# Row maxima of an attention unit moved once for all heads, by SyncE, with the transposed scores half a unit later

## The chip, the cores and the metric

One core of one Trainium2 chip runs the whole program as a single launch. The metric is device time in microseconds (us) from one run to the next of the same program: the median of the runs shown, lower is better. The profile below comes from one more execution, taken by the hardware profiler.

## The reference, cut to what matters

The input is 16 sequences of 256 tokens with 256 features and a context of the same shape. Five attention blocks (a0 to a4), three feed-forward blocks (f0, f1, f2) and a quantised linear layer (q8) run one after the other. Only attention is touched. Each block computes, for 16 heads of 16 columns (in a4: 8 heads of 64):

```python
scores = jnp.einsum('bhqd,bhkd->bhqk', q, k) / jnp.sqrt(hd)
attn = jax.nn.softmax(scores, axis=-1)      # a1 masks keys, a3 is causal
out = jnp.einsum('bhqk,bhkd->bhqd', attn, v)
return out @ w_proj + b_proj                # a0 has no projection
```

## The kernel before, in words

`attention` (line 75) takes one sequence as a unit, 16 units per block. Softmax subtracts the row maximum in a particular way. A unit's scores are computed twice on TensorE. First query rows lie on the partitions (`scores`, line 520); VectorE reduces each head to a negated row maximum in `NM` (lines 815 to 823). Then `NM` is transposed (entry `maxT`, line 633), ScalarE copies it to bf16 (`m_hi`, line 759), VectorE takes the rest (`m_lo`, line 924), and both parts are moved by DMA into spare rows of `QS`, the operand that holds the queries of all heads (lines 398 to 409). The second product, the transposed scores (`scoresT`, line 531), has these rows in its contraction and so gives scores minus maximum; ScalarE exponentiates it into `PT` (line 707), and `pv` multiplies with `VA`. `oT` transposes the head outputs back, VectorE normalises, `o2T` transposes again and `y` is the output projection.

Queries and keys reach `QS` and `KS` in the same way: the projections `q` and `k` are evacuated into `QH` and `KH`, and SyncE's function `move` (line 283) issues six DMAs for each, the two parts of every value into three row blocks. `QS` and `KS` have `B3 = 3` buffers, indexed by `u % 3`.

The order of all this is one list, `PLAN` (line 173), which each of the five engines walks in order. It is made of periods of 16 slots. In a period, role a (unit P) is projected, b (P-1) has its scores and maxima, c (P-2) its transposed scores, p (P-3) its tail, z (P+1) its statistics. An entry `sst` per head computes the scores of b's head and the transposed scores of c's head, in turn. `SLOTS` (line 115) places the rest. Before, `maxT` comes twice: for heads 0 to 7 of b at slot 9, and for heads 8 to 15 of c at slot 0. GpSimd issues four small DMAs for each half. TensorE waits for a half's four DMAs (`M`) at slot 0 and at slot 8 (line 565).

The waits that the steps touch, each in its engine's order:

```python
sp.wait_ge(S[name + "_lo"].sem, S[name + "_lo"].at(u, NB))              # 332, before move(u, q or k)
sp.wait_ge(S["st_ps"].sem, S["st_ps"].at(u - 3, NH))                    # 333
pe.wait_ge(S["q_moved"].sem, S["q_moved"].at(un, NQD))                  # 560, slot 0
pe.wait_ge(S["s_max"].sem, S["s_max"].at(un, i + 1 - 2))                # 562
pe.wait_ge(M.sem, M.at(uc, NMD * (i // (NH // 2)) + NMD))               # 565, slots 0 and 8
dve.wait_ge(S["o2T_ps"].sem, S["o2T_ps"].at(u - 1, NB))                 # 938
```

Line 333 holds back the copy of unit u's keys and queries until all transposed scores of unit u-3, which owns the same buffer, are computed. A block of SyncE's list is, in order: the context's store (slot 1), the keys' move (slot 3), the queries' move (slot 5), the next context's load (slot 10).

Of the kernel before, what the change touches and what calls it, by code (L numbers as in the profile page):

```python
# [4 lines left out]
P = 128  # L5
D = 256
BATCH = 16
SEQ = 256
# [66 lines left out]
def attention(nc, g, S, cfg):  # L75
# [27 lines left out]
               k_lo=NB, v_ps=NB, v_sb=NB, s_ps=NH, s_max=NH, mT_ps=2, m_hi=2, m_lo=2, st_ps=NH, p_ready=NH,  # L103
# [6 lines left out]
    M.begin(2 * NMD)  # L110
# [4 lines left out]
    def slots():  # L115
# [6 lines left out]
        put(0, "maxT", "c", 1)  # L122
# [9 lines left out]
        put(1, "pv", "p", 3)  # L132
# [71 lines left out]
    with ExitStack() as ctx:  # L204
# [13 lines left out]
        VA = sb("VA", [P, B3, 2, NH, VW], F32)  # L218
# [20 lines left out]
        MH = sb("MH", [NH // 2, 2, 2, SEQ], BF16)  # L239
# [29 lines left out]
        with nc.Block() as block:  # L269
            @block.sync  # L270
            def _(sp):
# [75 lines left out]
            def _(pool):  # L347
# [43 lines left out]
                for name, u, i, b, before in PLAN:  # L391
                    if name == "maxT":

                        pool.wait_ge(S["m_hi"].sem, S["m_hi"].at(u, i + 1))
                        pool.wait_ge(S["m_lo"].sem, S["m_lo"].at(u, i + 1))
                        if u == 0 and i == 0:
                            pool.wait_ge(S["const_ready"].sem, S["const_ready"].at(0, 4))
                        for part in range(2):
                            for j in range(2):
                                if wide:  # L400
                                    n = NH // 4
                                    dst = QS[WIDE_MAX + part:WIDE_MAX + part + 1, u % 3, 1,
                                             i * NH // 2 + j * n:i * NH // 2 + j * n + n, :]
                                    src = MH[j * n:j * n + n, i, part, :]
                                else:
                                    dst = QS[64 * j + MAXROW + part:64 * j + MAXROW + part + 1, u % 3, 0,
                                             4 * i:4 * i + 4, :]
                                    src = MH[4 * j:4 * j + 4, i, part, :]
                                nc.gpsimd.dma_start(dst, src).then_inc(M.sem, 16)  # L409
                    elif name == "stats":  # L410
# [78 lines left out]
            def _(pe):  # L489
# [61 lines left out]
                for name, u, i, b, before in PLAN:  # L551
# [4 lines left out]
                    elif name == "sst":  # L556
# [10 lines left out]
                        sbank, tbank = ps[:, i % 2, :], None if uc is None else ps[:, 2 + (uc * NH + i) % 3, :]  # L567
                        for t in range(2):
                            if un is not None:
                                ms = scores(un, i, t, sbank)  # L570
                            if uc is not None:
                                mt = scoresT(uc, order(i), t, tbank)
                        if causal:
                            for part in range(2):
                                if un is not None:
                                    ms = diagonal(i, g["tri_s"], part, 64 * part, P, sbank)
                                if uc is not None:
                                    mt = diagonal(order(i), g["tri_t"], part, 0, 64 * part + 64, tbank)
# [54 lines left out]
                    elif name == "maxT":  # L633
                        pe.wait_ge(S["s_max"].sem, S["s_max"].at(u, (i + 1) * NH // 2))
                        take(before)
                        for t in range(2):
                            m = nc.tensor.transpose(misc[:, t * P:t * P + P], NM[:, i, t, :], ident[:])
                        m.then_inc(S["mT_ps"].sem, 1)
                    elif name == "pv":
# [3 lines left out]
                        for t in range(2):  # L643
                            q0 = P if causal and t == 1 else 0
                            for j in range(HS):
                                h = i * HS + j
                                slot = order(h) % 8
                                if wide:
                                    a = (t * HS + j) * W
                                    for kt in range(2):  # L650
                                        m = nc.tensor.matmul(misc[:, a:a + VW],
                                                             PT[:, slot, kt * SEQ + t * P:kt * SEQ + t * P + P],
                                                             VA[:, u % 3, kt, h, :], start=(kt == 0), stop=(kt == 1))
                                else:
                                    m = nc.tensor.matmul(misc[32 * j:32 * j + 32, q0:SEQ], VA[:, u % 3, t, h, :],
# [32 lines left out]
            def _(act):  # L688
                for name, u, i, b, before in PLAN:
# [9 lines left out]
                    elif name == "sst" and before is not None:  # L699
                        uc = before  # L700
                        if uc == 0 and i == 0:
                            act.wait_ge(S["w_lo"].sem, S["w_lo"].at(nw - 1, 1))
                        act.wait_ge(S["st_ps"].sem, S["st_ps"].at(uc, i + 1))

                        act.wait_ge(S["pv_ps"].sem, S["pv_ps"].at(uc, (i - 8) // HS + 1))
                        n_ = SEQ + P if causal else 2 * SEQ
                        nc.scalar.activation(PT[:, i % 8, 0:n_], ps[:, 2 + (uc * NH + i) % 3, 0:n_],  # L707
# [34 lines left out]
                    elif name == "v":  # L742
                        act.wait_ge(S["v_ps"].sem, S["v_ps"].at(u, i + 1))

                        act.wait_ge(S["pv_ps"].sem, S["pv_ps"].at(u - 3, 4))
# [1553 lines left out]
```

## Time and profile before

| What | Value |
| --- | --- |
| Median of 3 runs | 3508.73 us (3496.87 to 3514.85) |
| Profiled execution | 3520.65 us, span 3518.8 us |
| PE busy | 2863.8 us (81%) |
| DVE busy | 2013.0 us (57%) |
| ACT busy | 1672.3 us (48%) |
| POOL busy | 1282.8 us (36%) |
| Mean granted TensorE clock | 0.905 |
| Scores of a0, a1, a2, a3, a4 run from / to | 41 to 345, 581 to 928, 1762 to 2076, 2132 to 2439, 2912 to 3412 us |

PE is TensorE, DVE VectorE, ACT ScalarE, POOL GpSimd, SP SyncE. A row of the timeline gives start, duration, engine, source line and operation, output<-input, shapes and count; behind it in brackets the engine's idle time before it and what ended that. The granted clock is 1.00 at 2.4 GHz and 0.50 at 1.2 GHz. Busy shares are means over stages with different limits.

### The profile page before, as it was taken

The page shows a single profiled execution, that of the slowest core. Times are in us where ns is not written, and L with a number is a line of the kernel's source. Part 1 is how long each engine was busy: PE and PEld are TensorE (multiplying, and loading weights), DVE is VectorE, ACT ScalarE, POOL GpSimd, SP SyncE. Part 2 cuts the span into 40 slices and gives each one's busy share as a digit, 9 for nine tenths or more (in the row PEclk, how much of TensorE's full clock was granted, in tenths as well). Part 3 has the DMA queues.
Part 4 walks back from the last instruction along what each step waited for, and adds up shares of the span by engine and source line. Part 5 has one row for each costly group of instructions (what it writes and reads, how often), then busy time and mean ns, then how long its engine had stood idle before and what let it go on. Part 6 is the DMA issues. An engine that isn't in the chain of part 4 may idle for free. (4 is left out here: it accounts for less than half of the span.)

```text
span 3518.8 us, 70742 instructions
## 1 busy us (share of the span) xinstructions
PE 2863.8 (81%) x26087; PEld 1916.9 (54%) x26206; DVE 2013.0 (57%) x4613; ACT 1672.3 (48%) x3112; POOL 1282.8 (36%) x1507
## 2 busy tenths in 40 slices
PE   5888676888789999999789877998219968999993
PEld 3554353454346666666545535665218855666672
DVE  4777554787655444433378765776814344555547
ACT  3777332666544444444257754665325523333332
POOL 6554006777200000000255546563350044555532
PEclk8999796999879999999889998999559978999995
DMA  3221002111114000000011101110233324323211
GB/s 112 71 69 53 13 1 79 62 63 61 49 56 139 1 1 1 1 1 1 28 54 58 54 32 40 46 41 28 83 127 91 96 88 100 70 67 81 60 34 48
DMA packets 211341, 190.00 MB, mean 54 GB/s; under 512 B 41840, under 2 KB 189568, under 8 KB 210848
## 3 DMA queue, kind: packets, MB, share of 16 engines
q1 hardware_dynamic: 184384, 167.44, 15.8%
q0 software_dynamic: 26624, 18.04, 2.0%
q8 instruction: 219, 3.59, 0.4%
q14 instruction: 114, 0.93, 0.1%
HBM read 67.09 MB, written 41.42 MB: 31 GB/s over the span
## 5 line engine op out<-in xcount | busy, mean ns | idle before, releaser
L1509 DVE TENSOR_TENSOR f1H<-f1HF,f1H 128x512 bf16<-128x512 f32 x256 | 176.7, 692 | 398.2 <-ACT f1H L1354 398.2
L1309 PE MATMUL ps<-f1w,f1H 128*128 128x256 bf16 x3072 | 379.2, 274 | 0.0
L1287 PE MATMUL ps<-f1xT,f1w 128*128 128x512 bf16 x1448 | 360.3, 384 | 12.3 <-ACT f1H L1354 6.1
L1309 PEld LDWEIGHTS ps<-f1w,f1H 128*128 128x128 bf16 x3072 | 301.9, 98 | 90.9 <-issue 1.7
L1351 ACT ACTIVATE f1HF<-ps 128x512 f32<-128x512 f32 x256 | 152.8, 597 | 333.9 <-PE ps L1287 333.8
L1287 PEld LDWEIGHTS ps<-f1xT,f1w 128*128 128x128 bf16 x1536 | 148.5, 99 | 152.7 <-issue 18.8
L1197 POOL TENSOR_TENSOR f1RS<-f1VE,neghalf 128x4 f32<-128x4 f32 x8 | 8.1, 1013 | 541.4 <-DVE f1VE L1492 541.4
L820 DVE TENSOR_REDUCE a0NM<-ps 128x2 f32<-128x512 f32 x256 | 166.4, 684 | 53.5 <-PE ps L526 53.2
L820 DVE TENSOR_REDUCE a1NM<-ps 128x2 f32<-128x512 f32 x256 | 166.4, 685 | 41.4 <-PE ps L526 40.6
L820 DVE TENSOR_REDUCE a2NM<-ps 128x2 f32<-128x512 f32 x256 | 166.0, 685 | 30.9 <-PE ps L526 28.9
L817 DVE TENSOR_REDUCE a3NM<-ps 128x1 f32<-128x128 f32 (+1 forms) x512 | 149.5, 350 | 43.2 <-PE ps L548 39.9
L707 ACT ACTIVATE a4PT<-ps 128x512 f32<-128x512 f32 x128 | 76.1, 597 | 194.9 <-PE ps L537 168.9
L707 ACT ACTIVATE a1PT<-ps 128x512 f32<-128x512 f32 x256 | 144.7, 595 | 37.8 <-PE ps L537 36.1
L707 ACT ACTIVATE a2PT<-ps 128x512 f32<-128x512 f32 x256 | 144.7, 595 | 35.4 <-PE ps L537 33.8
L707 ACT ACTIVATE a0PT<-ps 128x512 f32<-128x512 f32 x256 | 143.0, 598 | 35.0 <-PE ps L537 32.8
L472 POOL DMA_INDIRECT Y<-results,IX x64 | 63.4, 991 | 251.6 <-DMA results<-f2XS 234.4
L1354 ACT ACTIVATE f1H<-ps 128x512 bf16<-128x512 f32 x256 | 151.5, 592 | 0.0
L1920 DVE TENSOR_TENSOR f2XS<-f2XS 128x512 bf16<-128x512 f32 x78 | 54.0, 693 | 169.8 <-ACT f2XS L1780 169.8
L707 ACT ACTIVATE a3PT<-ps 128x384 f32<-128x384 f32 x256 | 117.5, 489 | 63.8 <-PE ps L548 60.9
L526 PE MATMUL ps<-a4KS,a4QS 128*128 128x256 bf16 (+1 forms) x512 | 129.5, 288 | 14.6 <-DMA a4QS<-a4QH 9.8
L409 POOL DMA_DIRECT2D a4QS<-a4MH x128 | 68.4, 540 | 191.6 <-DVE a4MH L924 182.7
L526 PE MATMUL ps<-a1KS,a1QS 49*128 49x256 bf16 x512 | 95.9, 286 | 48.9 <-DVE a1NM L820 19.1
(553 smaller groups left out, 7558.2 us busy)
## 6 DMA issues: line engine op xcount, KB each, us to landing
a4KS<-a4KH SPq DMA_DIRECT2D x96, 128.0 KB
a4QS<-a4QH SPq DMA_DIRECT2D x96, 128.0 KB
slots<-zeros SPq DMA_DIRECT2D x1, 9984.0 KB, 32.4
f2XS<-slots SPq DMA_DIRECT2D x39, 256.0 KB
results<-f2XS SPq DMA_DIRECT2D x39, 256.0 KB, 2.2
f1WF<-in_f_w SPq DMA_DIRECT2D x32, 256.0 KB, 2.7
f2WF<-in_f_w SPq DMA_DIRECT2D x16, 512.0 KB, 5.3
a0KS<-a0KH SPq DMA_DIRECT2D x96, 64.0 KB
```

What stands on the lines that cost most here:

```text
L409: nc.gpsimd.dma_start(dst, src).then_inc(M.sem, 16)
L472: nc.gpsimd.indirect_dma_start(GB[:, t % 4, k, :], None, g["results"][:, :], bass.IndirectOffsetOnAxis(ap=g["IX"][:, k, t:t + 1], axis=0)) ...
L526: m = nc.tensor.matmul(bank[:, at:at + keys], QS[r0:r1, u % 3, ch, gi, t * P:t * P + P], KS[r0:r1, u % 3, ch, gi, 0:keys], start=(ch == 0 ...
L707: nc.scalar.activation(PT[:, i % 8, 0:n_], ps[:, 2 + (uc * NH + i) % 3, 0:n_], ACT.Exp, scale=scale).then_inc(S["p_ready"].sem, 1)
L817: s_ = nc.vector.tensor_reduce(NM[:, hf, t, col:col + 1], bank[:, lo:hi], AX.X, MAX, negate=True)
L820: s_ = nc.vector.tensor_reduce(NM[:, hf, :, col:col + 1], bank.rearrange("p (t k) -> p t k", t=2), AX.X, MAX, negate=True)
L1287: m = nc.tensor.matmul(ps[:, (u * NCH + i) % 2, :], w1[:, x, kt, i * P:i * P + P], xT[:, half, y, kt, :], start=(j == 0), stop=(j == len(t ...
L1309: m = nc.tensor.matmul(out, H[:, (u * NCH + i) % HR, x, t * P:t * P + P], w2[:, y, i, :], start=first, stop=(f == YC - 1 and j == 2 and no ...
L1351: nc.scalar.activation(HF[:, (u * NCH + i) % 2, :], ps[:, (u * NCH + i) % 2, :], cfg["gelu"], **bias).then_inc(S["h_full"].sem, 1)
L1354: nc.scalar.activation(H[:, (u * NCH + i) % HR, 0, :], ps[:, (u * NCH + i) % 2, :], cfg["gelu"], **bias).then_inc(S["h_hi"].sem, 1)
L1509: nc.vector.tensor_tensor(H[:, (u * NCH + i) % HR, 1, :], HF[:, (u * NCH + i) % 2, :], H[:, (u * NCH + i) % HR, 0, :], SUB).then_inc(S["h_ ...
L1920: nc.vector.tensor_tensor(dst_[:, 1].rearrange("p f n -> p (f n)"), HF[:, half, :], dst_[:, 0].rearrange("p f n -> p (f n)"), SUB).then_in ...
```

## The change

The row maxima of a unit are transposed once, for all heads, at slot 1 of the period after its scores; `NM` and `MH` now alternate between two halves by unit. SyncE issues the four DMAs (all heads in each) instead of GpSimd's eight, and stands them in its list between the previous context load and the context store. The transposed scores move on by half a unit: heads 0 to 7 of c in slots 8 to 15, heads 8 to 15 of p in slots 0 to 7. What follows them moves by eight slots: `pv` to 13, 1, 5, 9; `oT` to 3 and 11; `o2T` from 5 to 13 (a4: 13, 14), `y` from 8 to slot 0 of the next period. `VA` gets a fourth buffer. Each block has one more period at its end (a4 has the same number). `B3` and line 333 stay as they are.

```diff
@@ signals @@
-               k_lo=NB, v_ps=NB, v_sb=NB, s_ps=NH, s_max=NH, mT_ps=2, m_hi=2, m_lo=2, st_ps=NH, p_ready=NH,
+               k_lo=NB, v_ps=NB, v_sb=NB, s_ps=NH, s_max=NH, st_ps=NH, p_ready=NH,
-    M.begin(2 * NMD)
+    M.begin(NMD)
@@ slots @@
-        put(0, "maxT", "c", 1)
+        put(1, "maxT", "c", 0)
         put(0, "xT", "a", 0)
-        put(1, "pv", "p", 3)
+        put(1, "pv", "p", 1)
         for i in range(NB):
             put(3 + i, "k", "a", i)
             put(5 + i, "q", "a", i)
             put(7 + i, "v", "a", i)
         if not wide:
-            put(3, "oT", "p", NO - 1)
+            put(3, "oT", "p", 0)
+            put(11, "oT", "p", NO - 1)
         if proj:
             for i in range(NB):
-                put(5 + i, "o2T", "p", i)
-        put(8, "y", "p", 0)
-        put(9, "maxT", "b", 0)
+                put(13 + i, "o2T", "p", i)
+        put(0, "y", "n", 0)
         if fin:
-            put(13, "fin", "p", 0)
-            put(6, "amax", "n", 0)
-        put(5, "pv", "c", 0)
-        put(9, "pv", "c", 1)
-        put(13, "pv", "c", 2)
-        if not wide:
-            put(11, "oT", "c", 0)
+            put(5, "fin", "n", 0)
+            put(14, "amax", "n", 0)
+        put(13, "pv", "c", 0)
+        put(5, "pv", "p", 2)
+        put(9, "pv", "p", 3)
@@ plan @@
-        for period in range(-2 if gather else -1, BATCH + (4 if fin else 3)):
+        for period in range(-2 if gather else -1, BATCH + 4):
-                if k % (16 // NH) == 0 and (live("b") or live("c")):
-                    made.append(("sst", unit["b"] if live("b") else None, k * NH // 16, None,
-                                 unit["c"] if live("c") else None))
+                if k % (16 // NH) == 0:
+                    i = k * NH // 16
+                    r = "c" if i >= NH // 2 else "p"
+                    if live("b") or live(r):
+                        made.append(("sst", unit["b"] if live("b") else None, i, None,
+                                     (unit[r], (i + NH // 2) % NH) if live(r) else None))
@@ buffers @@
-        VA = sb("VA", [P, B3, 2, NH, VW], F32)
+        VA = sb("VA", [P, 4, 2, NH, VW], F32)
-        MH = sb("MH", [NH // 2, 2, 2, SEQ], BF16)
+        MH = sb("MH", [NH, 2, 2, SEQ], BF16)
@@ sync; the maxT branch of gpsimd (lines 392 to 409) goes @@
+                    elif name == "maxT":
+                        sp.wait_ge(S["m_hi"].sem, S["m_hi"].at(u, 1))
+                        sp.wait_ge(S["m_lo"].sem, S["m_lo"].at(u, 1))
+                        if u == 0:
+                            sp.wait_ge(S["const_ready"].sem, S["const_ready"].at(0, 4))
+                        n = NH // 2
+                        for half in range(2):
+                            for j in range(2):
+                                if wide:
+                                    dst = QS[WIDE_MAX + half:WIDE_MAX + half + 1, u % 3, 1, j * n:j * n + n, :]
+                                else:
+                                    dst = QS[64 * j + MAXROW + half:64 * j + MAXROW + half + 1, u % 3, 0, :, :]
+                                sp.dma_start(dst, MH[j * n:j * n + n, u % 2, half, :]).then_inc(M.sem, 16)
@@ tensor, sst and maxT @@
-                            if i % (NH // 2) == 0:
-                                pe.wait_ge(M.sem, M.at(uc, NMD * (i // (NH // 2)) + NMD))
-                            pe.wait_ge(S["p_ready"].sem, S["p_ready"].at(uc, i + 1 - 3))
+                            uc, ic = uc
+                            if ic == 0:
+                                pe.wait_ge(M.sem, M.at(uc, NMD))
+                            pe.wait_ge(S["p_ready"].sem, S["p_ready"].at(uc, ic + 1 - 3))
-                        pe.wait_ge(S["s_max"].sem, S["s_max"].at(u, (i + 1) * NH // 2))
+                        pe.wait_ge(S["s_max"].sem, S["s_max"].at(u, NH))
-                            m = nc.tensor.transpose(misc[:, t * P:t * P + P], NM[:, i, t, :], ident[:])
+                            m = nc.tensor.transpose(misc[:, t * P:t * P + P], NM[:, u % 2, t, :], ident[:])
@@ scalar and vector, maxT @@
-                        if u:
-                            act.wait_ge(M.sem, M.at(u - 1, NMD * i + NMD))
-                        nc.scalar.activation(MH[:, i, 0, :], misc[0:NH // 2, 0:SEQ], ACT.Copy
+                        if u > 1:
+                            act.wait_ge(M.sem, M.at(u - 2, NMD))
+                        nc.scalar.activation(MH[:, u % 2, 0, :], misc[0:NH, 0:SEQ], ACT.Copy
-                        nc.vector.tensor_tensor(MH[:, i, 1, :], misc[0:NH // 2, 0:SEQ], MH[:, i, 0, :], SUB
+                        nc.vector.tensor_tensor(MH[:, u % 2, 1, :], misc[0:NH, 0:SEQ], MH[:, u % 2, 0, :], SUB
...
```

## Rows read from the trace of the kernel before

**Rows 1.** View of line 409, the DMAs of the maxima: who waited (us, times).
```profile
  PE ps L526: 58.6, 34
```
**Rows 2.** Timeline, TensorE, a0 to a3: first scores of period 3, then of period 16.
```profile
80.38 0.27 PE L526 MATMUL ps<-a0KS,a0QS 49*128 49x256 bf16 x1 [2.35 <-DMA a0QS<-a0MH]
...
332.27 0.27 PE L526 MATMUL ps<-a0KS,a0QS 49*128 49x256 bf16 x1 [0.47 <-DVE a0NM L820]
...
624.48 0.39 PE L526 MATMUL ps<-a1KS,a1QS 49*128 49x256 bf16 x1 [2.12 <-DMA a1QS<-a1QH]
...
913.17 0.27 PE L526 MATMUL ps<-a1KS,a1QS 49*128 49x256 bf16 x1 [0.45 <-DVE a1NM L820]
...
1801.29 0.27 PE L526 MATMUL ps<-a2KS,a2QS 49*128 49x256 bf16 x1 [2.40 <-DMA a2QS<-a2MH]
...
2059.96 0.27 PE L526 MATMUL ps<-a2KS,a2QS 49*128 49x256 bf16 x1 [1.39 <-DMA a2QS<-a2MH]
...
2167.60 0.21 PE L526 MATMUL ps<-a3KS,a3QS 49*128 49x128 bf16 x1 [0.88 <-DVE a3NM L817]
...
2424.67 0.21 PE L526 MATMUL ps<-a3KS,a3QS 49*128 49x128 bf16 x1 [0.41 <-DVE a3NM L817]
```
**Rows 3.** Timeline, TensorE: V product of period 3, right behind slot 7's scores.
```profile
90.82 1.38 PE L517 MATMUL ps<-a0wv,a0cT 128*128 128x256 bf16 x11
...
636.70 1.49 PE L517 MATMUL ps<-a1wv,a1cT 128*128 128x256 bf16 x12
...
1811.96 1.48 PE L517 MATMUL ps<-a2wv,a2cT 128*128 128x256 bf16 x12
...
2177.76 1.48 PE L517 MATMUL ps<-a3wv,a3xT 128*128 128x256 bf16 x12
```
**Rows 4.** Timeline, SyncE's queue in period 3: moves of keys and queries.
```profile
88.43 3.74 SPq L295 DMA_DIRECT2D a0KS<-a0KH  x6
92.27 5.07 SPq L295 DMA_DIRECT2D a0QS<-a0QH  x6
...
633.95 3.74 SPq L295 DMA_DIRECT2D a1KS<-a1KH  x6
637.74 1.43 SPq L340 DMA_DIRECT2D a1KS<-a1MROW  x2
639.28 4.54 SPq L295 DMA_DIRECT2D a1QS<-a1QH  x6
...
1809.24 4.05 SPq L295 DMA_DIRECT2D a2KS<-a2KH  x6
1813.41 3.74 SPq L295 DMA_DIRECT2D a2QS<-a2QH  x6
...
2174.68 4.53 SPq L295 DMA_DIRECT2D a3KS<-a3KH  x6
2179.32 3.73 SPq L295 DMA_DIRECT2D a3QS<-a3QH  x6
```
**Rows 5.** Timeline, start of a0: last move of queries, first scores behind it.
```profile
35.45 3.73 SPq L295 DMA_DIRECT2D a0QS<-a0QH  x6
...
41.00 0.61 PE L526 MATMUL ps<-a0KS,a0QS 49*128 49x256 bf16 x2 [8.14 <-DMA a0QS<-a0QH]
```
**Rows 6.** Windows: length, then five engines' busy, PEclk, DMA share, GB/s.
```profile
82.00:83.00 1.00, 1.00 (x14) 0.80 (x14) 0.83 (x4) 1.00 (x2) 0.33 (x1) 0.50 0.07 16
```
**Rows 7.** Timeline, TensorE, a2: transpose of maxima, transpose o2T, projection y.
```profile
1801.62 0.44 PE L637 MATMUL ps<-ident,a2NM 128*128 128x128 f32 x2
...
1809.82 0.66 PE L674 MATMUL ps<-ident,a2O 128*128 128x128 f32 x4
...
1813.70 1.48 PE L517 MATMUL ps<-a2wo,a2oT 128*128 128x256 bf16 x12
```
**Rows 8.** Page, costliest groups: exponentials of a2.
```profile
L707 ACT ACTIVATE a2PT<-ps 128x512 f32<-128x512 f32 x256 | 144.7, 595 | 35.4 <-PE ps L537 33.8
```
**Rows 9.** Timeline, TensorE, a4: V product behind a wait for VectorE.
```profile
3214.66 1.07 PE L517 MATMUL ps<-a4wv,a4cT 128*128 128x512 bf16 x3 [2.34 <-DVE a4O L944]
```

More of the change, by code:

```diff
@@ L391, in _ @@
                 for name, u, i, b, before in PLAN:
[L392 to L410, printed above, removed]
+                    if name == "stats":
                         h = u % 2
@@ L563, in _ @@
                         if uc is not None:
[L564 to L567 removed]
+                            uc, ic = uc
+                            if ic == 0:
+                                pe.wait_ge(M.sem, M.at(uc, NMD))
+                            pe.wait_ge(S["p_ready"].sem, S["p_ready"].at(uc, ic + 1 - 3))
+                        sbank, tbank = ps[:, i % 2, :], None if uc is None else ps[:, 2 + (uc * NH + ic) % 3, :]
                         for t in range(2):
@@ L571, in _ @@
                             if uc is not None:
-                                mt = scoresT(uc, order(i), t, tbank)
+                                mt = scoresT(uc, order(ic), t, tbank)
                         if causal:
@@ L577, in _ @@
                                 if uc is not None:
-                                    mt = diagonal(order(i), g["tri_t"], part, 0, 64 * part + 64, tbank)
+                                    mt = diagonal(order(ic), g["tri_t"], part, 0, 64 * part + 64, tbank)
                         if un is not None:
@@ L652, in _ @@
                                                              PT[:, slot, kt * SEQ + t * P:kt * SEQ + t * P + P],
-                                                             VA[:, u % 3, kt, h, :], start=(kt == 0), stop=(kt == 1))
+                                                             VA[:, u % 4, kt, h, :], start=(kt == 0), stop=(kt == 1))
                                 else:
-                                    m = nc.tensor.matmul(misc[32 * j:32 * j + 32, q0:SEQ], VA[:, u % 3, t, h, :],
+                                    m = nc.tensor.matmul(misc[32 * j:32 * j + 32, q0:SEQ], VA[:, u % 4, t, h, :],
                                                          PT[:, slot, t * SEQ:t * SEQ + SEQ - q0],
@@ L699, in _ @@
                     elif name == "sst" and before is not None:
-                        uc = before
-                        if uc == 0 and i == 0:
+                        uc, ic = before
+                        if uc == 0 and ic == 0:
                             act.wait_ge(S["w_lo"].sem, S["w_lo"].at(nw - 1, 1))
-                        act.wait_ge(S["st_ps"].sem, S["st_ps"].at(uc, i + 1))
-                        act.wait_ge(S["pv_ps"].sem, S["pv_ps"].at(uc, (i - 8) // HS + 1))
+                        act.wait_ge(S["st_ps"].sem, S["st_ps"].at(uc, ic + 1))
+                        act.wait_ge(S["pv_ps"].sem, S["pv_ps"].at(uc, (ic - 8) // HS + 1))
                         n_ = SEQ + P if causal else 2 * SEQ
-                        nc.scalar.activation(PT[:, i % 8, 0:n_], ps[:, 2 + (uc * NH + i) % 3, 0:n_],
+                        nc.scalar.activation(PT[:, ic % 8, 0:n_], ps[:, 2 + (uc * NH + ic) % 3, 0:n_],
                                              ACT.Exp, scale=scale).then_inc(S["p_ready"].sem, 1)
@@ L743, in _ @@
                         act.wait_ge(S["v_ps"].sem, S["v_ps"].at(u, i + 1))
-                        act.wait_ge(S["pv_ps"].sem, S["pv_ps"].at(u - 3, 4))
+                        act.wait_ge(S["pv_ps"].sem, S["pv_ps"].at(u - 4, 4))
                         if u == 0 and i == 0:
@@ L749, in _ @@
                         if NB == 1:
-                            dst = VA[:, u % 3].rearrange("p t h w -> p (t h) w")[:, :, 0:DH]
+                            dst = VA[:, u % 4].rearrange("p t h w -> p (t h) w")[:, :, 0:DH]
                         else:
-                            dst = VA[:, u % 3, i, :, 0:DH]
+                            dst = VA[:, u % 4, i, :, 0:DH]
                         nc.scalar.activation(dst, misc[:, :].rearrange("p (h w) -> p h w", w=DH), fn
@@ L805, in _ @@
                     elif name == "sst" and u is not None:
-                        if i % (NH // 2) == 0:
-                            dve.wait_ge(S["mT_ps"].sem, S["mT_ps"].at(u - 1, i // (NH // 2) + 1))
+                        if i == 0:
+                            dve.wait_ge(S["mT_ps"].sem, S["mT_ps"].at(u - 2, 1))
                         if u == 0 and i == 0:
@@ L811, in _ @@
                         dve.wait_ge(S["s_ps"].sem, S["s_ps"].at(u, i + 1))
-                        hf, at = i // (NH // 2), i % (NH // 2)
-                        col = at if wide else 4 * (at % 2) + at // 2
+                        col = i if wide else 8 * (i % 2) + i // 2
                         bank = ps[:, i % 2, :]
@@ L816, in _ @@
                             for t, (lo, hi) in enumerate(((0, P), (P, P + SEQ))):
-                                s_ = nc.vector.tensor_reduce(NM[:, hf, t, col:col + 1], bank[:, lo:hi],
+                                s_ = nc.vector.tensor_reduce(NM[:, u % 2, t, col:col + 1], bank[:, lo:hi],
                                                              AX.X, MAX, negate=True)
                         else:
-                            s_ = nc.vector.tensor_reduce(NM[:, hf, :, col:col + 1],
+                            s_ = nc.vector.tensor_reduce(NM[:, u % 2, :, col:col + 1],
                                                          bank.rearrange("p (t k) -> p t k", t=2),
```

## The prediction

> **What bounds the kernel now.** I read the page first: TensorE is busy 81% of the span, so a saving on another engine counts only where TensorE waits for it. The view of the line that issues the maxima's DMAs shows what this change aims at: TensorE stood 58.6 us, in 34 waits, before scores at slot 0 until a first half of maxima had landed [rows 1]. Then I cut the four blocks with 16 heads into periods by the scores that open each one. Periods 3 to 15 are the 13 in which every role has a unit. They last (332.27-80.38)/13 = 19.4 us in a0, (913.17-624.48)/13 = 22.2 in a1, (2059.96-1801.29)/13 = 19.9 in a2 and (2424.67-2167.60)/13 = 19.8 in a3 [rows 2]. TensorE's own work nearly fills them; the wait for maxima is one gap, the transfer of the next unit's queries ends close behind it.
>
> **The wait that the change moves.** SyncE may not copy unit u's keys and queries into `KS`/`QS` before all transposed scores of unit u-3 are done (line 333), because there are three buffers and u-3 owns the same one. Before, unit u-3 is finished in the period before, and this wait is free: the keys' move starts when `k_lo` is there, 8.1 us into period 3 of a0 (88.43-80.38) [rows 2, 4]. After, heads 8 to 15 of unit u-3 (role p) are computed in slots 0 to 7 of the same period in which u (role a) is projected. The buffer count stays three. So the keys' move, due at slot 3, now waits for slot 7, and behind it in SyncE's list stand the queries' move and the context load. TensorE's slot 0 of the next period waits for the queries. That closes a loop, and its length is a lower bound of the period:
>
> - From slot 0 to the end of slot 7's scores. The V product stands right behind them: 90.82-80.38 = 10.4 us in a0, 12.2 in a1, 10.7 in a2, 10.2 in a3 [rows 2, 3].
> - From the first issue of the keys' move to the end of the last of the queries': 97.34-88.43 = 8.9 us in a0, 7.9 in a2, 8.4 in a3, 9.9 in a1, which has two mask rows more [rows 4]. I take 8.4, the mean of the three, and 9.9 in a1.
> - From there to the scores: 35.45+3.73 = 39.18, the scores start at 41.00: 1.8 us [rows 5].
>
> In a0 nothing of the first half grows (one transpose of maxima stands in it before and after), so the loop is 10.4+8.4+1.8 = 20.6 us, 1.2 above the old period. In a1, a2 and a3 the projection y comes into the first half (+1.5) and o2T leaves it (-0.7) [rows 7]. TensorE would be ready near 17 to 19 us, so it stands some 3 us at every slot 0, and its clock falls after that: behind the wait of 2.35 us before 80.38 us, the clock is 0.50, that is 1.2 GHz, in the third microsecond [rows 2, 6]. Three of the four starts above stand behind such a wait of over 2 us; a3's stands behind 0.88 [rows 2], so it gets 0.6 more (an estimate: a few microseconds at half clock, much of it under waits for VectorE), and y at half clock gets 0.3 in all three. a1: 12.2+0.8+0.3, less an estimated 1 us of waiting at o2T that leaves the first half, is 12.3; with 9.9 and 1.8 that is 24.0, +1.8. a2: 10.7+0.8+0.3 = 11.8, +8.4+1.8 = 22.0, +2.1. a3: 10.2+0.8+0.6+0.3 = 11.9, +10.2 = 22.1, +2.3. Sum over four blocks 7.4 us a period, times 13 gated periods: **+96 us**. Bounds: with the shortest chain seen (7.9) and no fall of clock 0.5, 0.9, 1.0 and 1.1, together 3.5, times 13 = +46; with the longest (8.9) and a further 0.7 for y and the transposes at half clock 1.7, 2.3, 3.0 and 3.0, together 10, times 13 = +130.
>
> **What the change saves.** The 58.6 us of waits for maxima go in all blocks: the one remaining wait stands seven busy slots behind the transpose. In the 13 periods of a0 to a3 this saving is already inside the loop, since the old mean contains the waits and the loop replaces them. So is the second transpose, 0.44 us on TensorE [rows 7], and one small operation each on ScalarE and VectorE. GpSimd loses eight issues a unit; it is idle half the time in these blocks and nobody waits for it there, so that is worth nothing. On SyncE four issues come in ahead of the keys' move; two mask rows of the same shape take 1.43 us [rows 4], so four take 2.9 us. They start some 4 us into the period and end near 7, when the keys' move stands at its wait for slot 7 anyway: nothing, and landing 1.8 us later they are there before slot 8. If the gate were not there they would push the keys by up to 0.5 us.
>
> **Fill and drain.** Each block's last eight heads have their exponentials half a period later with nothing beside them: 8 x 0.595 = 4.8 us [rows 8]. At the other end the first half of period 2 has no transposed scores and two `pv` fewer, worth 2 to 3 us, and the ungated starts lose a wait for maxima. I take 0 for the five blocks together; bounds -15 (drain hidden) and +24 (no gain at the fill, 5 x 4.8).
>
> **a4.** With 8 heads a period lasts about 33 us, and slot 6, its last gated head, comes near 16 us with y in front; keys and queries are then there before 30 us, so the gate should just not bind. TensorE waits there 2.34 us for the normalisation behind the first `pv` [rows 9], which waits for o2T of the unit before. That pair goes to slots 13 and 14, with scores and a transpose before the next user of the bank. I take 10 us less (0.8 a period), from 0.7 us for one transpose and its gap; bounds -35 (the whole wait and its clock go, in all periods) and +15 (the gate binds by 1 us).
>
> **Sum.** +96 +0 -10 = +86 on the profiled execution, 3520.65 to 3607 us. The runs' median is 12 us lower than that execution, 3508.73; so I predict **3595 us**.
>
> **The rule that speaks against this.** The rows say that issuing is what fills the chain: 12 DMAs take 7.9 to 8.9 us of SyncE's queue, against 1.8 us until the last has landed [rows 4, 5]. The Trainium skill, "DMA: Bandwidth & Descriptors", section "Issuing engines are not separate DMA queues", says that the sequencer's time for starting a DMA is usually small beside the transfer itself. By that rule the chain would shrink to the transfers, the gate would be hidden, and the result would be rival 1 below. The trace does not agree here, and I give the rule only that rival's chance.
>
> **Rivals.**
>
> 1. *The late start is hidden* and the waits for maxima simply go: faster. It needs keys and queries in place within about 8 us of slot 7, while the rows give 10.2. Then a period falls by its share of the 58.6 us and by one transpose of 0.44 us with its gap of 0.2: 58.6+80x0.6 = 107 at most. The queries' landing takes over part of it (in a0's period 3 the old chain ends at 97.34+1.8 = 99.1, 18.8 us into a period of 19.4). So -60: 3449. It decides only if SyncE's chain is under 8 us. Chance 0.07.
> 2. *The gate binds, at its low bound*: chain 7.9, clock kept. +46-10-5 = +31: 3540. For it: a3 shows no slow start behind 0.88 us, so a short wait may leave the clock alone. Against: the wait would be about 2 us or more. Chance 0.20.
> 3. *The gate binds in a4 too*, and half-clock stretches cost more: +120 (near the high bound) +15 = +135: 3644. For it: a4's moves are twice as large and its slack is only some 2 us. Chance 0.13.
> 4. *Savings and gate cancel*: loop +2 us in a1 to a3 is wrong because y only fills waits that TensorE has for VectorE in the first half, and a4 gains its full 35 us: +46-35-5, about +6: 3515. Chance 0.07.
>
> **How the numbers follow.** The forecast has 0.53, its own range 3562 to 3630. The 80% range must take in rival 2 and most of rival 3; it leaves out rival 1 and 4 and the far end of 3: 3527 to 3650. A measurement here can tell about 0.5% (17.5 us) from no change. Slower by more: forecast, 2 and 3 and a little of 4, 0.87. Faster by more: rival 1 nearly whole, 0.07. The rest 0.06.
>
> **What would show it.** After the change, the first issue of the keys' move should stand right behind the last scores of slot 7 in periods 3 to 15, and behind `k_lo` in periods 0 to 2. Every slot 0 from period 4 on should have TensorE waiting 2 to 4 us for the queries' DMA, with 0.50 clock behind it, and no wait for the maxima. Periods: a0 20.6, a1 24.0, a2 22.0, a3 22.1, a4 near 32. Blocks whose periods are shorter than before would prove me wrong, as would a keys' move that starts at slot 4.

## The result, and the profile after

The changed kernel takes 3622.61 us (median of 6 runs, 3599.99 to 3626.48) where the kernel before takes 3506.64 (6 runs, 3496.87 to 3514.85): a ratio of 1.0324, 95% interval 1.0294 to 1.0354. It is slower by 116 us; 3595 was predicted, with a range of 3527 to 3650. Five of the six runs of the changed kernel lie between 3621 and 3627 us, the sixth is the 3599.99.

The profiled execution took 3621.40 us, span 3619.3, granted clock 0.887 (0.905 before). TensorE is busy 2900.2 us (80%), VectorE 1988.9, ScalarE 1659.0, GpSimd 946.8. The first scores of a unit are the groups in which TensorE's idle time grew; behind the bar stand busy time, mean ns, then TensorE's idle time before the group and what ended most of it. The kernel before, for a2, then the changed kernel, for a1, a0 and a2:

```profile
L526 PE MATMUL ps<-a2KS,a2QS 49*128 49x256 bf16 x512 | 93.0, 281 | 43.1 <-DVE a2NM L820 22.4 <-DMA a2QS<-a2MH 10.5 <-DMA a2QS<-a2QH 8.1
```
```profile
L522 PE MATMUL ps<-a1KS,a1QS 49*128 49x256 bf16 x512 | 94.1, 291 | 91.1 <-DMA a1QS<-a1QH 72.5
...
L522 PE MATMUL ps<-a0KS,a0QS 49*128 49x256 bf16 x512 | 92.2, 288 | 61.1 <-DMA a0QS<-a0QH 53.0
...
L522 PE MATMUL ps<-a2KS,a2QS 49*128 49x256 bf16 x512 | 92.6, 288 | 54.7 <-DMA a2QS<-a2QH 45.0
```

Before, the queries' move ended 11.3, 15.7 and 8.1 us of it in a0, a1 and a2, now 53.0, 72.5 and 45.0. TensorE stands before the first scores of a period for the move of the queries, and for the maxima hardly any more (four waits in a0 to a3, 4.1 us in all, against [rows 1]). From period 4 to 16 every one of the 52 first scores of a period stands behind a wait for the queries, of 2.1 to 5.0 us. In TensorE's timeline, the first scores of period 3 and of period 16, as in [rows 2]:

```profile
79.40 0.28 PE L522 MATMUL ps<-a0KS,a0QS 49*128 49x256 bf16 x1 [2.56 <-DMA a0QS<-a0QH]
...
346.63 0.28 PE L522 MATMUL ps<-a0KS,a0QS 49*128 49x256 bf16 x1 [3.39 <-DMA a0QS<-a0QH]
...
643.57 0.28 PE L522 MATMUL ps<-a1KS,a1QS 49*128 49x256 bf16 x1 [2.57 <-DMA a1QS<-a1QH]
...
965.61 0.39 PE L522 MATMUL ps<-a1KS,a1QS 49*128 49x256 bf16 x1 [4.31 <-DMA a1QS<-a1QH]
...
1859.37 0.37 PE L522 MATMUL ps<-a2KS,a2QS 49*128 49x256 bf16 x1 [0.56 <-DVE a2NM L815]
...
2136.69 0.39 PE L522 MATMUL ps<-a2KS,a2QS 49*128 49x256 bf16 x1 [2.73 <-DMA a2QS<-a2QH]
...
2251.36 0.23 PE L522 MATMUL ps<-a3KS,a3QS 49*128 49x128 bf16 x1 [1.50 <-DMA a3QS<-a3QH]
...
2535.49 0.28 PE L522 MATMUL ps<-a3KS,a3QS 49*128 49x128 bf16 x1 [2.73 <-DMA a3QS<-a3QH]
```

Thirteen periods take 267.2 us in a0 (20.6 each), 322.0 in a1 (24.8), 277.3 in a2 (21.3) and 284.1 in a3 (21.9). Before they took 251.9, 288.7, 258.7 and 257.1 [rows 2]. That is +15.3, +33.4, +18.6 and +27.1, together **+94.4 us**; the prediction had +96. (A second profiled execution of the kernel before, in the experiments, has 258.6, 287.4, 258.9 and 257.7 us; against it the loop costs 88 us.) The cause shows in SyncE's queue and in TensorE's V product, which stands right behind slot 7's scores:

```profile
85.76 0.44 SPq L341 DMA_DIRECT2D ctx_T<-a0cT  x1
90.08 3.83 SPq L296 DMA_DIRECT2D a0KS<-a0KH  x6
94.01 4.23 SPq L296 DMA_DIRECT2D a0QS<-a0QH  x6
```
```profile
89.89 1.49 PE L513 MATMUL ps<-a0wv,a0cT 128*128 128x256 bf16 x12
...
100.07 0.28 PE L522 MATMUL ps<-a0KS,a0QS 49*128 49x256 bf16 x1 [3.24 <-DMA a0QS<-a0QH]
```

SyncE stands still from 86.20 to 90.08, while the split keys are ready at about 87.4, and issues the keys' first DMA 0.2 us after slot 7's scores. It does so in all 52 periods from 3 to 15 of a0 to a3, never earlier. 8.2 us of issue and 1.8 us of landing later (94.01+4.23 = 98.24, scores at 100.07) TensorE goes on. Below, this wait of the moves for the end of slot 7 is called the gate.

Now the whole program. The start of a block is its memset of `KS` (or the first statistics of f0 to f2), so the blocks' lengths in us are:

| block | before | after | difference |
| --- | --- | --- | --- |
| a0 | 353.2 | 373.2 | +20.0 |
| a1 | 409.4 | 450.3 | +40.9 |
| a2 | 372.0 | 395.7 | +23.7 |
| a3 | 368.0 | 401.5 | +33.5 |
| a4 | 593.7 | 575.5 | -18.2 |
| f0, f1, f2 | 1346.5 | 1347.0 | +0.5 |

The four blocks grow by 118.1 us, 94.4 of them in the 13 periods. The other 23.7 lie at their ends. From a block's start to period 3 it is 1.0, 1.1, 2.2 and 0.2 us shorter (-4.5); from period 16 to the next block it is 5.7, 8.6, 7.2 and 6.7 us longer (+28.2).

### The profile page after: what moved, and what is told of

Same layout as the page of the kernel before. It is cut to its first block and busy times, and to the rows that moved or that the text cites. A ratio compares the mean times of both kernels' runs of the same rounds, so it can differ in the third digit from the quotient of the medians.

```text
span 3619.3 us, 69662 instructions
## 1 busy us (share of the span) xinstructions
PE 2900.2 (80%) x26046; PEld 1937.3 (54%) x26046; DVE 1988.9 (55%) x4533; ACT 1659.0 (46%) x3032; POOL 946.8 (26%) x867
## 3 DMA queue, kind: packets, MB, share of 16 engines
q1 hardware_dynamic: 188992, 168.62, 15.7%
## 5 line engine op out<-in xcount | busy, mean ns | idle before, releaser
L1282 PE MATMUL ps<-f1xT,f1w 128*128 128x512 bf16 x1536 | 380.0, 384 | 5.9 <-ACT f1H L1349 5.9
L522 PE MATMUL ps<-a1KS,a1QS 49*128 49x256 bf16 x512 | 94.1, 291 | 91.1 <-DMA a1QS<-a1QH 72.5
L522 PE MATMUL ps<-a0KS,a0QS 49*128 49x256 bf16 x512 | 92.2, 288 | 61.1 <-DMA a0QS<-a0QH 53.0
L522 PE MATMUL ps<-a2KS,a2QS 49*128 49x256 bf16 x512 | 92.6, 288 | 54.7 <-DMA a2QS<-a2QH 45.0
```

The source lines that it names most:

```text
L522: m = nc.tensor.matmul(bank[:, at:at + keys], QS[r0:r1, u % 3, ch, gi, t * P:t * P + P], KS[r0:r1, u % 3, ch, gi, 0:keys], start=(ch == 0 ...
L1282: m = nc.tensor.matmul(ps[:, (u * NCH + i) % 2, :], w1[:, x, kt, i * P:i * P + P], xT[:, half, y, kt, :], start=(j == 0), stop=(j == len(t ...
```

## The experiments

Block lengths in us, each from one profiled execution, and the time of each kernel. The kernel before, timed beside them, had medians of 3527.6 (first four kernels), 3503.3 (next four) and 3524.9 us (last four); the first eight kernels ran on one chip, the last four on another, so it moved by 24 us on one and the same chip. Single block lengths move too: with the same code a0 of the kernel before took 353.2 and 364.8 us, and with a fourth buffer that nothing waits for 357.1, and a3 368.0, 367.7 and 378.8. So up to some 12 us in a0 or a3 of a single profile may be chance; a1 (409.4 to 410.0) and a2 (372.0 to 372.1) repeat.

| kernel | a0 | a1 | a2 | a3 | a4 | median | ratio (95%) |
| --- | --- | --- | --- | --- | --- | --- | --- |
| four buffers | 343.0 | 406.1 | 352.9 | 357.8 | 579.5 | 3462.0 | 0.9815 (0.9794, 0.9837) |
| before + gate | 372.9 | 434.0 | 385.6 | 391.7 | 572.7 | 3592.0 | 1.0189 (1.0165, 1.0213) |
| queries by GpSimd | 359.0 | 403.5 | 366.0 | 363.8 | 583.6 | 3497.9 | 0.9922 (0.9898, 0.9945) |
| y late | 378.6 | 432.9 | 375.3 | 375.4 | 582.1 | 3566.7 | 1.0111 (1.0086, 1.0135) |
| four buffers + GpSimd | 334.7 | 388.8 | 351.9 | 353.7 | 580.8 | 3431.9 | 0.9803 (0.9784, 0.9822) |
| before + four buffers | 357.1 | 409.5 | 372.1 | 378.8 | 569.8 | 3507.9 | 1.0014 (1.0005, 1.0024) |
| four buffers + y late | 339.3 | 389.3 | 361.0 | 358.6 | 583.6 | 3459.2 | 0.9865 (0.9842, 0.9887) |
| before + gate, y first | 376.2 | 458.0 | 409.7 | 414.2 | 569.9 | 3649.4 | 1.0411 (1.0392, 1.0430) |
| before, again | 364.8 | 410.0 | 372.1 | 367.7 | 589.6 | 3529.6 | one run |
| both cures, a4 as before | 334.2 | 385.4 | 352.6 | 352.7 | 589.4 | 3440.9 | 0.9763 (0.9744, 0.9783) |
| both cures, again | 334.0 | 389.2 | 352.1 | 353.7 | 583.8 | 3432.3 | 0.9735 (0.9717, 0.9753) |
| four buffers, again | 344.4 | 403.5 | 352.1 | 360.3 | 582.1 | 3458.6 | 0.9810 (0.9792, 0.9828) |

**1. The changed kernel with four buffers.**

```diff
-    B3 = 3
+    B3 = 3 if wide else 4
-                        sp.wait_ge(S["st_ps"].sem, S["st_ps"].at(u - 3, NH))
+                        sp.wait_ge(S["st_ps"].sem, S["st_ps"].at(u - B3, NH))
```
(and `u % B3` for `u % 3` wherever `QS` and `KS` are indexed)

> The changed kernel with QS and KS in four buffers in a0 to a3 (a4 keeps three), so that the moves of unit u wait for the transposed scores of unit u-4, long done. Theory (the late gate on the moves, then 12 DMAs issued one after the other by SyncE, is what lengthens the periods): the waits for queries at slot 0 go (before the change there were none), the four blocks fall from 373, 450, 396 and 402 us to at or below the 353, 409, 372 and 368 us of before, because the waits for maxima are gone too: about 3450 us in all, between 3420 and 3500. Rival (the new order itself costs, as TensorE's y first in the period and both halves of the maxima moved at once): the blocks keep at least half of their gain in length, 3560 us or more.

3462.0 us: without the gate the loss is gone, so the gate is the cause. a0, a2 and a3 fall below their old lengths by 10, 19 and 10 us (experiment 11 repeats all four lengths within 3 us). a1 hardly does, by 3 us. The page's row says why: the queries' DMA still ends 39.5 us of idle time there, where it ended 15.7 before the change (so there were some such waits before, other than the expectation says). With the mask's two, 14 DMAs follow one another there once the keys are split; a second queue beside the four buffers (experiment 5) takes the 39.5 down to 17.9.

```profile
L522 PE MATMUL ps<-a1KS,a1QS 49*128 49x256 bf16 x512 | 91.0, 283 | 56.1 <-DMA a1QS<-a1QH 39.5
```

**2. The kernel before with the gate alone.**

```diff
                         sp.wait_ge(S["st_ps"].sem, S["st_ps"].at(u - 3, NH))
+                        sp.wait_ge(S["st_ps"].sem, S["st_ps"].at(u - 2, NH // 2))
```

> The kernel before with one more wait of SyncE, ahead of the moves of keys and queries of unit u: for the transposed scores of the first half of the heads of unit u-2, which is the point of the period (end of slot 7) from which the changed kernel lets them start. All else is as before. Theory: this alone gives most of the loss; the moves are issued from about 9 to 10 us of the period on, queries land at about 20, periods of a0 to a3 grow by 1 to 2 us and the waits for maxima stay: 3560 to 3640 us, 3600 likeliest. Rival (the lateness of the moves is covered, the loss is from other parts of the change): 3500 to 3520 us.

3592.0 us. A single wait, with nothing else changed, makes a0 to a3 longer by 19.7, 24.6, 13.6 and 23.7 us, 81.6 in all (69 against the second profile of the kernel before), and the median 64 us longer, with the same signature in the page:

```profile
L527 PE MATMUL ps<-a1KS,a1QS 49*128 49x256 bf16 x512 | 96.5, 291 | 64.4 <-DMA a1QS<-a1QH 54.6
```

The expectation had the waits for maxima stay. They nearly go (2 in a0, 2 in a3): TensorE now arrives after them. This is what the forecast meant by a saving that is inside the loop.

**3. Queries moved by GpSimd.**

```diff
-                        move(u, name)                  # sync
+                        if name == "k":
+                            move(u, name)
...
+                    if name == "q" and i == NB - 1:    # gpsimd, same waits, same six DMAs
+                        move(u, name)
```

> The changed kernel with the six DMAs of the queries' move issued by GpSimd, with the same waits, while SyncE issues the six of the keys. Theory (the chain from the gate to the first scores is mostly issue time: 12 DMAs in about 8 us, landing 1.8 us behind the last): with two queues it is 4 to 6 us for each, both at once, so the waits of 2.7 to 5 us at slot 0 shrink to below 2: 3620 less 13 periods times 2 us times four blocks, about 3520 us, between 3480 and 3570. Rival (by the Trainium skill's page DMA: Bandwidth & Descriptors, section Issuing engines are not separate DMA queues, it is the transfers that fill this time, and another issuing engine adds nothing): 3600 to 3640 us.

3497.9 us, 3.4% below the 3622.6 of the changed kernel, with the gate still in place. The timeline of a2, GpSimd's row first, then SyncE's, then TensorE's next first scores:

```profile
1824.25 3.12 POOL L418 DMA_DIRECT2D a2QS<-a2QH  x6 [2.80 <-DVE a2QH L929]
...
1823.49 4.20 SPq L296 DMA_DIRECT2D a2KS<-a2KH  x6
...
1832.39 0.27 PE L545 MATMUL ps<-a2KS,a2QS 49*128 49x256 bf16 x1 [1.52 <-DMA a2KS<-a2KH]
```

The two sets of six, one behind the other for 8 us before, lie beside each other. Windows over the chain, with the mean busy share of the 16 DMA engines as the last but one number: the changed kernel in a0 (issuing the keys' move, then the queries', as above), then this kernel in a2 (issuing both, then landing):

```profile
90.00:94.00 4.00, 4.00 (x48) 2.35 (x46) 3.07 (x6) 3.48 (x8) 0.00 (x0) 1.00 0.20 69
94.00:98.20 4.20, 2.52 (x33) 0.87 (x32) 3.63 (x7) 3.00 (x6) 0.00 (x0) 1.00 0.28 94
```
```profile
1823.50:1827.70 4.20, 4.20 (x52) 2.31 (x50) 3.68 (x7) 3.49 (x8) 3.43 (x7) 1.00 0.47 114
1827.70:1832.30 4.60, 2.73 (x36) 1.27 (x32) 4.05 (x8) 3.32 (x7) 0.96 (x1) 1.00 1.03 130
```

While SyncE issued the 12 alone, the DMA engines were a fifth to a quarter busy, so it was issuing that filled the chain. With two queues that no longer holds: issuing takes 4.2 us in place of 8.2, but from the end of SyncE's issue (1823.49+4.20 = 1827.69) to the scores it is 4.7 us in place of 1.8, and the DMA share is 1.03. The chain, from the keys' first issue to the scores, is 8.9 us here and 10.0 in the rows of the changed kernel (90.08 to 100.07). This run speaks against the rule weighed in the prediction (the Trainium skill, "DMA: Bandwidth & Descriptors", section "Issuing engines are not separate DMA queues") for these DMAs of 64 KB. What TensorE now waits for is the keys, 1.5 us, and the mean period of a2 is 19.4 us in place of 21.3. About half of these 1.9 us is the shorter chain; the other half lies in slots 0 to 7, where the V product comes at 10.0 us or earlier in 12 of 13 periods, against 10.0 or 10.1 in 6 of 13 in the changed kernel and up to 12.8 in the others (see y and the clock, below).

**4. y of a1 to a3 late** (`put(9, "y", "n", 0)` behind the scores of slot 9, in place of slot 0).

> The changed kernel with the output projection y of a1, a2 and a3 put at the end of slot 9, behind the gate's last head, in place of slot 0. Theory (the period of a1 to a3 is a loop: first scores, slots 0 to 7, gate, moves, first scores; so what TensorE does in slots 0 to 7 lengthens it, and what it does behind slot 7 is hidden by the issue of the moves): each of some 13 periods of three blocks is shorter by the 1.3 to 2.6 us that y took there, together 50 to 100 us: 3520 to 3570 us; a0 and a4 don't move. Rival (TensorE's total work or a fixed latency sets the period): 3600 to 3640 us, since no work is taken away.

3566.7 us. No work is taken away, and a1 is 17.4 us shorter, a2 20.5, a3 26.1, together 64 us, so these blocks are loops through the gate. (The median is 56 us lower.) a0, whose code is the same, came out 5 us longer: that much is spread between executions. In the 13 periods it is 1.4, 1.4 and 1.9 us a period. y itself also takes longer at slot 0, 2.0 us a unit in a2 in place of 1.55, because there it runs at a fallen clock in nine of its 16 units. Groups of a2 between 1700 and 2480 us, first in the changed kernel, then in this one:

```profile
L513 PE MATMUL ps<-a2wo,a2oT 128*128 128x256 bf16 x192 | 32.6, 336 | 1.5 <-ACT a2oT L765 1.5
```
```profile
L516 PE MATMUL ps<-a2wo,a2oT 128*128 128x256 bf16 x192 | 24.8, 281 | 1.5 <-ACT a2oT L768 1.5
```

**5. Four buffers and GpSimd together** (edits 1 and 3). One thing is not in the sum of the two: the wait of GpSimd's move is still for unit u-3, so here the keys are free of the gate and the queries are not.

> The changed kernel with both cures at once: QS and KS in four buffers in a0 to a3, and the queries' moves issued by GpSimd. With four buffers a1 still waited 1.3 to 3.3 us a period for its queries, a0 1.1 to 2.0 us, because the 12 DMAs of one period begin only when the keys are split; a2 and a3 hardly waited. Theory: the second queue takes those waits away: a0 343 us to about 335, a1 406 us to about 385, a2 and a3 unmoved; 3420 to 3445 us where the kernel with four buffers alone took 3462, a ratio to before of 0.970 to 0.977. Rival: TensorE is by now full in these periods, and a wait that goes comes back as another one: a ratio of 0.979 to 0.984.

The block lengths do what the theory said (a0 334.7, a1 388.8), and 3431.9 us is 30 below experiment 1, yet the ratio, 0.9803, is what the rival said (0.979 to 0.984), since the kernel before ran faster that time. Experiments 10 and 11 settle it. The gate that is left costs next to nothing: the split queries are ready 9.5, 12.1, 10.4 and 10.2 us into the usual period of a0 to a3, and slot 7's scores are done at 9.5, 11.7, 10.0 and 10.3.

**6. The kernel before with four buffers.**

> The kernel before with QS and KS in four buffers in a0 to a3, nothing else changed. Theory: in the kernel before the wait of the moves for unit u-3 ended long before the keys were split, so a fourth buffer gives nothing: a ratio of 0.996 to 1.004; the gain of the changed kernel with four buffers (0.9815) is then the gain of the change's own order. Rival: the fourth buffer itself gives part of that gain: 0.98 to 0.99.

1.0014: 0.14%, and not a gain. So the fourth buffer earns its time only in the changed order, and what experiment 1 gains over the kernel before is the order's own gain.

**7. Four buffers and y late** (edits 1 and 4).

> The changed kernel with four buffers of QS and KS, and y of a1 to a3 at the end of slot 9 too. Moving y there without the fourth buffer gave about 75 us. Theory: that was because y lay ahead of the gate, inside the loop; with the gate free y costs TensorE the same wherever it stands: a ratio as with four buffers alone, 0.978 to 0.986. Rival: y at the period's start is dear in itself (it stands ahead of the keys' projection, so it delays the moves even without the gate, and it runs at the low clock): 0.965 to 0.975.

3459.2 us, as four buffers alone (3462.0 and 3458.6), so the theory holds for the sum; the ratio, 0.9865, is a little above what it allowed. (One of its four runs took 11703 us; nothing recorded says why, and the ratio is of the other three.) But it is not true block by block: a1 is 17 us shorter, for y no longer delays the keys (their move starts 8.3 us into the period, in experiment 1 at 9.5 to 10.4), and a2 8 us longer, which stays open. The gain of y late without the fourth buffer, which the expectation puts at 75 us, was 64 in the blocks of experiment 4.

**8. The kernel before with the gate and y first** (edit 2, and y at slot 0 of the next period in a1 to a3).

> The kernel before with the gate at the end of slot 7 (as in the run with the gate alone, 1.019) and y of a1 to a3 put at slot 0 of the next period, which is where the changed kernel has it. Theory: gate and y ahead of it make up nearly the whole loss of the changed kernel (1.032): each period of a1 to a3 grows by 1 to 2 us more, 50 us in all: a ratio of 1.028 to 1.040. Rival: what is left is from other parts (the maxima moved at once, the V products): 1.015 to 1.023, as with the gate alone.

1.0411, just above the range: a1, a2 and a3 are 24, 24 and 22 us longer than with the gate alone, 20 to 21 of it in the 13 periods, 1.5 to 1.6 us each. They are also longer than in the changed kernel, which has only one transpose of maxima and no wait for a second half. So gate and y first explain more than the loss. That the rest of the change gives some of it back follows from the difference; no run shows which part does.

**9 to 12. a4, and the two cures side by side.** One more execution of the kernel before:

> The kernel before once more, unchanged, for another profiled execution of it. In the profile of before most periods of a4 took 33.9 us at a granted clock of 0.95 and a few 30.8 at 1.00; in the profiles of three experiments that leave a4's order as before, all took 30.8 to 30.9, and a4 570 to 573 us instead of 594. Theory: the 34 us periods are a chance of that execution, and a4 of the kernel before usually takes about 570 to 573 us, so that the changed order costs a4 some 5 us and doesn't save 18. Rival: they belong to the kernel before, and the experiments' a4 was shortened by how they enter it: 590 us or more here too.

589.6 us: the theory fell, or half of it. a4 in the order of before has two lengths, 589 to 594 us (the profile of before, this one, the next) and 570 to 573 (experiments 2, 6 and 8). Windows of one period each, two of the kernel before, then one of experiment 6 (length, five engines' busy time, clock, DMA share, GB/s):

```profile
3129.80:3163.80 34.00, 31.41 (x234) 22.36 (x234) 18.00 (x46) 11.88 (x24) 18.21 (x22) 0.95 0.31 71
...
3231.50:3262.40 30.90, 29.84 (x234) 22.05 (x234) 18.00 (x46) 11.88 (x24) 18.24 (x22) 1.00 0.33 78
```
```profile
3100.00:3130.80 30.80, 29.96 (x234) 21.96 (x233) 17.89 (x46) 11.83 (x23) 18.09 (x22) 1.00 0.33 78
```

> Four buffers of QS and KS, the queries' moves issued by GpSimd, the changed order in a0 to a3, and a4 wholly as in the kernel before (its order, its half maxima moved by GpSimd, V in three buffers). Theory: a4 takes 570 to 573 us in place of 581, nothing else moves: 8 to 11 us less than the kernel with the two cures alone on this chip, a ratio some 0.003 below it. Rival (the 34 us periods are a4's own in this order): a4 590 us or more, a ratio 0.003 or more above it.

3440.9 against 3432.3 us: with a4 as before the kernel is 8.5 us slower here (3.3 by the spans of the profiles), and its a4 took the long form, 589.4 us. So the rival's number nearly came true (0.0028 in the ratio), but its reason isn't shown: in experiments 2, 6 and 8 the same order was short.

> The kernel with both cures again (four buffers, queries' moves by GpSimd), beside the one with four buffers alone on the same chip, as the two were timed on different chips. Theory, from the block lengths of their profiles (334.7, 388.8, 351.9, 353.7, 580.8 against 343.0, 406.1, 352.9, 357.8, 579.5 us): 29 us less than it, 0.008 in the ratio. Rival: the ratios of the two chips are right, and there is 0.002 at most between them.

> The changed kernel with four buffers of QS and KS alone, on the chip of the run with both cures. Theory: 25 to 33 us above that one. Rival: within 8 us of it.

3432.3 and 3458.6 us on one chip: 26 us apart, as the blocks said. That is what experiment 11 expected (25 to 33). Both kernels repeat their own time of the other chip within 4 us, so the chip isn't what parted the ratios of experiments 1 and 5; those two had been timed on one chip, other than the expectation says. It is the kernel before that moved, between 3503 and 3528. The 20 us between its two a4 lengths would be enough for it, but a4 isn't recorded in those runs, so that is likely and not shown.

## Why the prediction was right, and where its size was off

- **The wait that the change moves.** Shown, by taking it out (experiment 1), by adding it alone (2) and by the chain in SyncE's queue. Periods of 20.6, 24.8, 21.3 and 21.9 us stand against 20.6, 24.0, 22.0 and 22.1 predicted; +94.4 against +96. It is right in the sum, with errors both ways in a1 and a2, and that it is right to 2 us is luck: against the second profile of the kernel before it is +88. In a1 the V product comes 12.4 to 13.8 us into the period from period 4 on, where 12.3 was taken; in a2 it comes at 11.1 in the mean, where 11.8 was taken. The bounds of +46 and +130 don't follow quite from the terms given (with a chain of 7.9 and no fall of clock the terms give some +51); the result lies well inside either way.
- **y and the clock.** The prediction expected a clock of 0.50 behind every wait at slot 0. It comes behind some. In a2 y takes 1.47 us in seven units and 2.3 to 2.8 in nine, so the 0.3 us taken for y at half clock measured 0.5 in the mean (2.04 against 1.55 in experiment 4). The periods of the two rows below last 19.6 and 23.2 us:

```profile
1902.79 1.47 PE L513 MATMUL ps<-a2wo,a2oT 128*128 128x256 bf16 x12
```
```profile
1943.27 2.77 PE L513 MATMUL ps<-a2wo,a2oT 128*128 128x256 bf16 x12
```
```profile
1903.30:1904.30 1.00, 1.00 (x11) 0.72 (x11) 0.80 (x4) 0.71 (x1) 0.00 (x0) 1.00 0.00 0
...
1943.40:1944.40 1.00, 1.00 (x7) 0.69 (x6) 0.81 (x4) 0.89 (x1) 0.00 (x0) 0.50 0.00 0
```

  They stand behind waits of 3.08 and 2.68 us for the queries. Why the clock stays at 1.00 behind the longer wait and falls to 0.50 (1.2 GHz) behind the other isn't settled.
- **What the change saves.** Right: four waits for maxima are left, and the four DMAs on SyncE delay nothing.
- **Fill and drain. This step failed.** "I take 0 for the five blocks together" should have been +23.7 in a0 to a3 alone, as much as its upper bound for all five (+24). The last heads' 4.8 us were seen, but a gain at the fill was set against them. The fill gave 0.2 to 2.2 us a block, the drain cost 5.7 to 8.6. The order brings this and not the gate: with four buffers the drain is still 4.9, 8.7, 4.6 and 5.2 us longer than before, with the gate alone it is 2.9 us in all. By the plan, the last eight heads bring not only their exponentials but their transposed scores and V products, with neither scores nor projections of another unit beside them; how the 5.7 to 8.6 us divide among these wasn't measured. Against the second profile of the kernel before the +23.7 are +18.
- **a4.** -10 predicted, -18.2 in the profile, both on top of a long a4 before. Where a4 in the order of before takes 570 to 573 us, the new order, 575 to 584 in all eight profiles, costs 3 to 14. Most of the 2.34 us wait in [rows 9] went with the long form and not with the order: experiment 6 waits 0.6 there, with the same order.
- **From the profiled execution to the median.** 12 us were taken off for both kernels. But the profile of before holds the long a4 and its runs, 14 us lower, mostly did not, it seems (their a4 isn't recorded); the changed kernel's profile and median agree within 1.2 us. Between the profiles the difference is +101, between the medians +116; that would be the reason. So the miss of 27.6 us is +23.7 of fill and drain, +13 of base, -8 of a4, -1.6 of loop, and 0.5 of the rest. Part of it cancels: the base and a4 were both read from one long execution.
- **Rival 1 was priced well for another kernel.** If the late start were hidden, 3449 us was the estimate, 60 below. Four buffers take it away, and experiment 1 has a ratio of 0.9815, that is 65 us of 3507. The closeness is luck in part: the estimate had no term for the longer drain (+23.3 in experiment 1), and the 13 periods gave 64.8.

## What to carry to other kernels

A change of order moves every wait on a buffer's last reader: list them, and for each ask in which slot the last reader now stands and how many DMA issues are queued behind the wait. Here one more buffer (8 KB a partition) turned +3.2% into -1.9%, and a second issuing queue beside it made it -2.7% (0.9735; 0.9803 beside the faster runs of the kernel before), the fastest kernel of these runs. A period that passes through a gate is a loop, and only the work ahead of the gate counts in it; work behind it is free as long as it fits beside the chain (experiment 4). A change that shifts work to a later stage also lengthens each block's end, here by 5.7 to 8.6 us a block.

## What had not been expected of the hardware

- **The second queue issues faster and lands later.** Six DMAs of 64 KB take 3.12 us on GpSimd in a2 (0.52 each) and 3.7 to 5.1 on SyncE; the prediction had no price for it. From issue to landing it is the other way round, a median of 4.1 us on GpSimd against 2.6 on SyncE (the last number of these rows, of the changed kernel and of experiment 3):

```profile
a2QS<-a2QH SPq DMA_DIRECT2D x96, 64.0 KB, 2.6
```
```profile
a2QS<-a2QH POOLq DMA_DIRECT2D x96, 64.0 KB, 4.1
```

  In experiment 3 the keys' six are issued at the same time, and no run has GpSimd issue without them, so how much of the 4.1 us is GpSimd's own path and how much the company isn't separated. GpSimd had the time for it: it is busy 36% of the span in the kernel with both cures.
- **Two lengths of one block.** In the long form of a4 ScalarE, and often VectorE with it, go on late. In the timeline of the kernel before, TensorE's transposes start at 3211.72 and take 0.60 us; ScalarE and VectorE, which wait for TensorE, start 1.6 us after that. "remote" in the brackets means that the profile names no releaser on this core:

```profile
3211.72 0.60 PE L674 MATMUL ps<-ident,a4O 128*128 128x128 f32 x4
...
3213.88 0.84 ACT L735 ACTIVATE a4QH<-ps,a4bq 128x256 bf16<-128x256 f32 x2 [2.68 <-remote]
3213.95 0.42 DVE L944 TENSOR_TENSOR a4O<-ps,a4RC 128x256 f32<-128x256 f32 x1 [4.46 <-remote]
```

  ScalarE has eight waits of this kind in a4 of this execution, six or seven in the other two long ones, and none in experiments 2, 6 and 8. VectorE has nine in this one and at most one in the others. The clock is only half of the matter. In the second profile of the kernel before five periods of a4 last 32.1 to 32.3 us, 1.5 us over the 30.8 of the short form; the row below has a clock of 1.00 and TensorE busy 30.0 us, as in the short form. Four others last 33.7 to 34.2 us; there the clock is 0.95 and TensorE busy 1.5 us longer. One of each kind:

```profile
3135.40:3167.70 32.30, 30.02 (x234) 22.02 (x233) 17.93 (x46) 11.82 (x23) 18.14 (x22) 1.00 0.31 74
...
3264.70:3298.50 33.80, 31.54 (x234) 22.31 (x232) 17.92 (x46) 11.83 (x23) 18.12 (x22) 0.95 0.31 71
```

  What delays the two engines stays open; nothing here was made to test it.
